# Three token tiles of the output projection moved from the token stage into the attention drain

## The reference

```python
h = s4d_kernel(x)                      # 16 sequences, 128 rows of 1024
h = concatenate([h, txt], axis=1)      # 16 x 205 rows (3280 tokens) of 1024
# attention: 32 heads of 32, one shared k and v head, alibi, causal
h = h + attn(layernorm(h)) @ Wo        # Wo 1024 x 1024
# token mixer: base layer and low rank experts with a router
x = layernorm(h)
logits = x @ router_W.T + router_b     # 15 routes
w = top 8 of softmax(logits), mapped to 8 experts
h = h + x @ base_W.T + base_b + sum_e w_e * 2 * (x @ A_e.T) @ B_e.T
```

## Time and profile before

| | before |
|---|---|
| median of 3 runs | 1673.88 us (1671.83 to 1674.54) |
| the profiled execution | 1673.85 us |
| its span, first to last instruction | 1672.1 us |
| PE busy | 1471.7 us (88%) |
| DVE busy | 1137.9 us (68%) |
| ACT busy | 735.7 us (44%) |
| POOL busy | 514.7 us (31%) |
| mean granted TensorE clock | 0.96 |
| DMA | 139.81 MB |

### The profile page before, as it was taken

One profiled execution on the slowest core, in us unless ns is written; L12 is line 12 of the kernel. 1 busy time (PEld: TensorE's weight loads), 2 busy tenths in 40 slices (PEclk: granted clock), 3 DMA queues, 4 the chain that ended last, 5 costly groups with the idle time before them and its releaser, 6 DMA issues. The chain is left out here.

```text
span 1672.1 us, 28883 instructions
## 1 busy us (share of the span) xinstructions
PE 1471.7 (88%) x9700; PEld 1315.2 (79%) x9700; DVE 1137.9 (68%) x4142; ACT 735.7 (44%) x2624; POOL 514.7 (31%) x314
## 2 busy tenths in 40 slices
PE   0264479999999999999999779999999999999999
PEld 0264478788888888887887558998999989899997
DVE  7999268989898988888879754453444435444443
ACT  3364229688787878786878631101101110111100
POOL 2687214444444444453445401010101101011010
PEclk9878789999999999999998789999999999999999
DMA  6134545546465646365555341212112121121211
GB/s 207 38 76 106 115 86 83 111 71 119 77 122 82 117 72 120 65 117 87 90 119 93 103 166 38 76 39 74 62 51 75 38 75 50 63 75 38 76 38 37
DMA packets 110522, 139.81 MB, mean 84 GB/s; under 512 B 13156, under 2 KB 96484, under 8 KB 110040
## 3 DMA queue, kind: packets, MB, share of 16 engines
q1 hardware_dynamic: 110408, 138.41, 36.8%
HBM read 62.82 MB, written 40.30 MB: 62 GB/s over the span
## 5 line engine op out<-in xcount | busy, mean ns | idle before, releaser
L735 ACT ACTIVATE P<-P,nmax 128x128 f32<-128x128 f32 (+1 forms) x1024 | 434.6, 426 | 86.3 <-DVE nmax L823 82.4
L797 POOL TENSOR_TENSOR P<-P,rden 128x512 f32<-128x512 f32 (+1 forms) x256 | 330.3, 1312 | 404.8 <-DVE rden L829 404.5
L823 DVE CUSTOM_DVE_ANT_0 P<-sc,mask 128x128 f32<-128x128 f32 (+1 forms) x1024 | 292.1, 323 | 73.1 <-PE sc L630 68.2
L1161 POOL TENSOR_TENSOR h<-h,base_b 128x1024 f32<-128x1024 f32 (+1 forms) x26 | 63.0, 2422 | 640.0 <-DVE xn L1188 640.0
L660 PE MATMUL pr<-xT_hi,wq_hi 128*128 128x410 f32 x576 | 242.8, 421 | 0.6 <-DVE xT_lo L839 0.6
L835 DVE COPY PTR<-pt 128x282 f32<-128x282 f32 x512 | 220.6, 432 | 14.2 <-PE pt L640 13.1
L1072 PE MATMUL b<-w_hi,x2T_hi 128*128 128x390 f32 (+3 forms) x624 | 214.6, 344 | 1.0 <-DVE x2T_lo L1198 1.0
L1072 PE MATMUL b<-w_lo,x2T_hi 128*128 128x390 f32 (+3 forms) x624 | 212.9, 341 | 0.0
L1072 PE MATMUL b<-w_hi,x2T_lo 128*128 128x390 f32 (+3 forms) x624 | 212.6, 341 | 0.0
L660 PE MATMUL pr<-xT_lo,wq_hi 128*128 128x410 f32 x576 | 201.4, 350 | 0.0
L660 PE MATMUL pr<-xT_hi,wq_lo 128*128 128x410 f32 x576 | 200.4, 348 | 0.0
(11 more groups left out here) (174 smaller groups left out, 3005.6 us busy)
## 6 DMA issues: line engine op xcount, KB each, us to landing
Qs<-q_hi SPq DMA_DIRECT2D x128, 205.0 KB, 4.8
Qs<-q_lo SPq DMA_DIRECT2D x64, 205.0 KB, 5.7
att_dram<-att SPq DMA_DIRECT2D x64, 205.0 KB, 2.8
at<-att_dram SPq DMA_DIRECT2D x25, 512.0 KB, 4.5
h<-h_dram SPq DMA_DIRECT2D x25, 512.0 KB, 3.4
out<-h SPq DMA_DIRECT2D x25, 512.0 KB, 2.6
h_dram<-Y SPq DMA_DIRECT2D x64, 128.0 KB, 3.0
ht<-h_dram SPq DMA_DIRECT2D x16, 512.0 KB, 6.1
```

Of the source, the lines that this page charges most:

```text
L735: last = nc.scalar.activation(P[rows, j % 2, i, cols], P[rows, j % 2, i, cols], ACT.Exp, scale=-1.0, bias=nmax[at], accum_out=den[at])
L797: lastp = nc.gpsimd.tensor_tensor(w, w, r, ALU.mult)
L823: lastv = v.tensor_tensor_reduce(P[0:n, j % 2, i, cols], sc[i % 2][0:n, cols], mask[0:n, m], 1.0, 3.0e38, ALU.add, ALU.min, nmax[0:n, j % ...
L1161: nc.gpsimd.tensor_tensor(h2[0:n, par, :], h2[0:n, par, :], base_b[0:n, :], ALU.add).then_inc(biased, 1)
```

## The change

Attention's output projection of tiles 0, 1 and 2 (384 tokens, all of them of the first two sequences) is computed in the drain of the attention block. Each of the 48 turns from turn 4 of the drain takes three matmuls of 512 columns (`out_step`); a half tile takes eight turns. For it `at` is loaded, split into `aT` (views of the buffers of xT, which are free after the last main product), the residual is loaded into `ht`, the sum is added there by DVE (`add_half`) and stored back to `h_dram`. So that Wo is there in time, it is read in column blocks, in the order of the main products, and each block is split into the place of a block of Wq that has been used: seven of the nine in the last pair, two slots behind the main product, two in the drain. The token stage goes over tiles 3 to 25 first and then over 0, 1 and 2, which skip the projection. `turn_z` stands in front of `transpose_x` in bodies without a projection, and `RESIDUAL_AFTER` is 2.

```diff
+EARLY = 3
+TILES_OUT = FULL + 1
+LATER = TILES_OUT - EARLY
...
-    WO_PIECES = KC + 1
-    SPLIT_AT = [1, 2, 3, 4] + [32, 33, 34, 35, 44]
+    WO_PIECES = len(MAIN)
+    WO_RING = 4
+    SPLIT_AT = [GH * (n + 2) + 2 for n in range(7)] + [GH * SLOTS + 2, GH * SLOTS + 5]
...
-        turn = GH * slot + i - after
-        return SPLIT_AT.index(turn) if last is None and turn in SPLIT_AT else None
+        turn = GH * slot + i - after + (GH * SLOTS if last is None else 0)
+        return SPLIT_AT.index(turn) if last in (True, None) and turn in SPLIT_AT else None
+
+    OUT_FROM, HALVES = 4, 2 * EARLY
+    A_HI_AT, A_LO_AT = [0, 12, 28], [1, 14, 30]
+    RES_SLOT = [1, 2, 3]
+    aT = [[w[:, :, r * 128:(r + 1) * 128] for w in xT] for r in range(2)]
...
+            def load_wo(n):
+                if n >= WO_RING:
+                    sp.wait_ge(wo_lo, n - WO_RING + 1)
+                if MAIN[n] == "kv":
+                    src = io["BT"].rearrange("p (k m) -> p k m", k=KC)
+                else:
+                    j = MAIN[n][1]
+                    src = io["Wo"].rearrange("(k p) m -> p k m", p=128)[:, :, 128 * j:128 * j + 128]
+                sp.dma_start(wo_stage(n), src).then_inc(wo_loaded[n], 16)
...
+            def store_res(t):
+                sp.wait_ge(half_read, 2 * t + 2)
+                sp.dma_start(io["h_dram"][t * 128:(t + 1) * 128, :], ht[:, RES_SLOT[t], :]).then_inc(res_stored, 16)
...
+                    if last is True and 3 <= slot < 3 + WO_PIECES - WO_RING:
+                        load_wo(slot + WO_RING - 3)
+                    if last is True and slot == 6:
+                        for q in att_stored:
+                            sp.wait_ge(q, 16 * 2 * UNITS // 2)
+                        for t in range(2):
+                            load_at(t, t, ta_loaded[t])
+                    if last is True and slot == 8:
+                        sp.wait_ge(wo_lo, 6)
+                        load_res(0)
                     if last is None and slot == 1:
...
+                        sp.wait_ge(ta_lo, 1)
+                        load_at(2, 0, ta_loaded[2])
+                        sp.wait_ge(wo_lo, 8)
+                        for t in (1, 2):
+                            load_res(t)
+                    if last is None and slot == 3:
+                        store_res(0)
+                        sp.wait_ge(ta_lo, 2)
+                        load_at(EARLY + 1, 1, W["a_loaded"][1])
                     if last is None and slot == 5:
...
+                        store_res(1)
+                        sp.wait_ge(ta_lo, 3)
+                        load_at(EARLY, 0, W["a_loaded"][0])
...
+            store_res(2)
+            sp.wait_ge(res_stored, 16 * EARLY)
...
+            def out_step(half, k):
+                t = half // 2
+                if k == 0:
+                    if half % 2 == 0:
+                        pe.wait_ge(ta_lo, t + 1)
+                    if half < 2:
+                        pe.wait_ge(wo_lo, (5, WO_PIECES)[half])
+                    if half < BANKS:
+                        pe.wait_ge(main_read, SLOTS * PAIRS - 2 + half)
+                    else:
+                        pe.wait_ge(half_read, half - BANKS + 1)
+                cols = slice(512 * (half % 2), 512 * (half % 2) + 512)
+                for m, (a, b) in enumerate(((0, 0), (0, 1), (1, 0))):
+                    last = nc.tensor.matmul(pr[half % BANKS][:, 0:512], aT[t % 2][a][:, k, :], wq[b][:, k, cols],
+                                            start=(k == 0 and m == 0), stop=(k == KC - 1 and m == 2))
...
+            def add_half(half):
+                t, cols = half // 2, slice(512 * (half % 2), 512 * (half % 2) + 512)
+                dve.wait_ge(half_done, half + 1)
+                dve.wait_ge(res_loaded[t], 16)
+                v.tensor_tensor(ht[:, RES_SLOT[t], cols], pr[half % BANKS][:, 0:512], ht[:, RES_SLOT[t], cols], ALU.add).then_inc(half_read, 1)
...
-    RESIDUAL_AFTER = 4
+    RESIDUAL_AFTER = 2
...
-                if n1 and not first:
+                ahead = n1 and not first and attends(t + 1)
+
+                def turns():
+                    if not ahead:
+                        turn_z(t, n)
+                    if n1:
+                        transpose_x(t + 1, n1, 0)
+                if ahead:
                     attn_out(t + 1, 1 - par, n1, between=lambda: turn_z(t, n))
                 wait_count(pe, out_ready, t)
                 three(base_ps[1], n, xT, w2, slice(*CHUNKS[1]), KC, stop=False)
-                if first or not n1:
-                    turn_z(t, n)
-                three(base_ps[2], n, xT, w2, slice(*CHUNKS[2]), KC, stop=False, between_at=TURN_AT,
-                      between=(lambda: transpose_x(t + 1, n1, 0)) if n1 else None)
+                three(base_ps[2], n, xT, w2, slice(*CHUNKS[2]), KC, stop=False, between_at=TURN_AT, between=turns)
```

More of the change, by code:

```diff
@@ L468, in attention_block @@
     rows_ready = sem("rows_ready")
+    ta_loaded, res_loaded = [sem(f"ta_loaded{i}") for i in range(EARLY)], [sem(f"res_loaded{i}") for i in range(EARLY)]
+    ta_hi, ta_lo, half_done, half_read, res_stored = sem("ta_hi"), sem("ta_lo"), sem("half_done"), sem("half_read"), sem("res_stored")
     wo_hi, wo_lo = sem("wo_hi"), sem("wo_lo")
@@ L718, in body @@
                             main_step(p, slot, main, i)
+                        if last is None and out_half(slot, i)[0] is not None:
+                            out_step(*out_half(slot, i))
                         chunk, pair = ln_chunk(slot, i, 0), ln_pair(p, slot, first, last)
@@ L737, in exp_head, with a_hi @@
                 last.then_inc(exp_done, 1)
+            def a_hi(t):
+                act.wait_ge(ta_loaded[t], 16)
+                if t >= 2:
+                    act.wait_ge(half_done, 2 * (t - 1))
+                nc.scalar.activation(aT[t % 2][0], W["at"][:, t % 2], ACT.Copy).then_inc(ta_hi, 1)
             def hi_ln(p, i):
@@ L773, in body @@
                             act.wait_ge(wo_loaded[k], 16)
-                            nc.scalar.activation(part_of(W["wq_hi"], k), ht[:, k % 4, :], ACT.Copy).then_inc(wo_hi, 1)
+                            nc.scalar.activation(part_of(W["wq_hi"], k), wo_stage(k), ACT.Copy).then_inc(wo_hi, 1)
+                        if last is None and GH * slot + i in A_HI_AT:
+                            a_hi(A_HI_AT.index(GH * slot + i))
                         if i == 6 and aj is not None:
@@ L905, in body @@
                             dve.wait_ge(wo_hi, k + 1)
-                            v.tensor_tensor(part_of(W["wq_lo"], k), ht[:, k % 4, :], part_of(W["wq_hi"], k).bitcast(F32),
+                            v.tensor_tensor(part_of(W["wq_lo"], k), wo_stage(k), part_of(W["wq_hi"], k).bitcast(F32),
                                             ALU.subtract).then_inc(wo_lo, 1)
+                        if last is None and GH * slot + i in A_LO_AT:
+                            a_lo(A_LO_AT.index(GH * slot + i))
+                        if last is None and out_half(slot, i, 1)[1] == KC - 1:
+                            add_half(out_half(slot, i, 1)[0])
                         if i == RECIP_AT[1] and tj is not None:
@@ L1014, in mlp_block @@
     out_stored = [sem("out_stored0"), sem("out_stored1")]
-    LAST = FULL
     def visit(eng, body):
-        size = lambda t: 128 if t < FULL else (REST if t == FULL else 0)
-        pairs = (FULL - 2) // 2
-        for t in range(2):
-            body(t, t % 2, t // 2, 128, 128, 128)
+        size = lambda u: 0 if u > FULL else (REST if u == LATER - 1 else 128)
+        pairs = (LATER - 3) // 2
+        for u in range(2):
+            body(u, u % 2, u // 2, 128, 128, 128)
         with eng.Fori(1, pairs) as i:
@@ L1025, in visit, with attends, row0 @@
                 body(i * 2 + par, par, i, 128, 128, 128)
-        for t in range(2 * pairs, FULL + 1):
-            body(t, t % 2, t // 2, size(t), size(t + 1), size(t + 2))
+        for u in range(2 * pairs, FULL + 1):
+            body(u, u % 2, u // 2, size(u), size(u + 1), size(u + 2))
+    def attends(u):
+        return not isinstance(u, int) or u < LATER
+    def row0(u):
+        return ((u + EARLY) if attends(u) else (u - LATER)) * 128
     with nc.Block() as block:
@@ L1224, in body @@
             def body(t, par, half_t, n, n1, n2):
-                link = Chain(dve, chain, LINKS * t + (5 + RSQRT_LINKS), setup)
+                fewer = 0 if attends(t) else t + 1 - LATER
+                link = Chain(dve, chain, LINKS * t + (5 + RSQRT_LINKS) - fewer, setup)
                 router(t, n, link)
```

55 lines of the change are left out of this document (30 added, 25 removed).

## The result

The changed kernel runs at **1686.2 us** (median of 4 runs, 1684.47 to 1689.79) against 1674.2 for the kernel before on the same chip: 1.0074 times its time, 95% interval 1.0062 to 1.0087. Forecast were 1677.8 and, as the range, 1668.5 to 1684.0. Of faster, same and slower, slower had the highest chance; the size was wrong, and the time lies outside the range.

A forecast was written before the change was run, and what follows sets the result against it. The prediction took PE's chain, mostly base product `b` and output projection `wo`, as the bound. Last pair 3.5, drain 12.1, start 1.2, projections -33.6, tail gaps 16.2 and clock 4.5 sum to +3.9: 1677.8 us, range 1668.5 to 1684.

The forecast's parts named there:

- Last pair: Slots 2 to 8 of attention's last pair: seven early Wo splits cost 0.5 us each, +3.5 us.
- 8.2 as the upper bound: Last pair: seven splits at 2.21 us, each us of DVE work lengthening the slot by 0.53, give 8.2 us.
- Rival (c): Last pair: splits stretch against POOL, each taking 2.21 us, pair grows by 8.2; 1682.5 us; chance 0.10.
- Drain: Attention's drain to the first `wo`, with 48 projection steps and turns of 1.16 us: +12.1 us.
- 0.5 for `a_lo` in DVE's order: Drain: 0.5 us added to PE's end for the place of `a_lo` in DVE's order.
- (d): Drain: the low clock stays, a turn takes about 2.0 us instead of 1.16; 1685 us; chance 0.10.
- (e): Drain: projection steps don't use idle PE, all 33.6 us come on top; 1699 us; chance 0.02.
- Start of the token stage: First `b` 3.2 us earlier, low clock +1.7, later `turn_z` of the first tile +2.7: net +1.2 us.
- Tail: Token stage's last three tiles with non-attending successors: 5.4 us PE idle each, +16.2 us, and low clock behind, +4.5.
- (a): Drain and new gaps: the clock isn't lost, taking back 8.8 us; 1669.0 us, faster; chance 0.18.
- (b): Last pair: DVE's 1.50 us idle per slot hide all splits; 1674.3 us; chance 0.15.
- the gain of 33.6 us: Token stage: three projections fewer at 11.2 us of PE each, -33.6 us.

The follow-up runs named there:

- split at turn 1: Changed kernel with DVE's low split of each Wo piece five turns later, at turn 1 of the next slot: 1687.4 us, 1.0079 of the kernel before.
- the run with `turn_z` early: Changed kernel with turn_z between the second and last third of the base product in bodies without a projection: 1673.3 us, 0.9994 of the kernel before.
- the run with the splits alone: Changed kernel without the projection in the drain, token stage as before, early Wo loads and splits kept: 1677.3 us, 1.0020 of the kernel before.
- the run with halves: Changed kernel with each low Wo split on DVE cut into two halves, the second two turns later: 1684.2 us, 1.0060 of the kernel before.
- statistics early: Changed kernel with `turn_z` early, plus layernorm statistics of a next tile without projection before DVE's wait for zT: 1664.1 us, 0.9932 of the kernel before.
- three edits: Changed kernel with low splits on GpSimd, `turn_z` early and next tile's layernorm statistics before the wait for zT: 1656.1 us, 0.9887 of the kernel before.

## Why the prediction was wrong

**Last pair, the step that failed.** "I take 0.5 us each, 3.5", with 8.2 as the upper bound; measured 9.9. Two things were wrong in it. The sum of DVE's work ("the sum of the DVE work fits": 1.50 us idle, a split of 1.47) is not the test: of DVE's 1.50 us idle in slot 2 of before, 1.36 lie ahead of the bias of turn 7, the split in the middle of a dense row of biases and copies, and what counts is whether PE's lead of two heads covers the instruction. I had named this lead and priced it at half a microsecond; a split of 1.2 us costs 0.84 (split at turn 1), and the run with the splits on GpSimd shows that nothing else costs anything by itself. And the upper bound took 0.53 us of slot per us of DVE from layernorm statistics one pair earlier, which are many short instructions; a single long one costs 1.35/1.88, 0.72 per us.

Rival (c), at 0.10, had one half of the mechanism, the stretch beside POOL: with the measured 9.9 in place of its 8.2 its 1682.5 becomes 1684.2, but no split took the 2.21 us that it gave to each (1.23 to 1.88), and it left out the cost without a stretch. DVE's timeline of before, the idle time of slot 2 and the split of 2.21 us:

```profile
850.72 0.29 DVE L823 CUSTOM_DVE_ANT_0 P<-sc,mask 128x128 f32<-128x128 f32 x1 [1.36 <-PE sc L630]
...
947.93 2.21 DVE L906 TENSOR_TENSOR wq_lo<-ht,wq_hi 128x1024 fp32r<-128x1024 f32 x1
```

I had read that split as lying in POOL's 3.54 us. It didn't: POOL ended at 949.06, the split at 950.14, 1.08 us later, so the rows of before already showed the wait that the last section works out.

Slots 6 and 7 carry 4.5 of the 9.9: in slot 6 the split waited 0.97 us for ACT, which I had put at 0.05 us free, and PE's granted clock was 0.88, and 0.95 in slot 7. That clock loss in the pair wasn't in my sum at all. The trace shows it beside the waits; no run separates it from them.

**Drain.** +12.1 forecast, +10.2 measured. A turn of 1.16 us (930.45 to 931.68 is one of 1.23; the next are 1.15 to 1.17), the first step 5.2 us after `q_hi`, 6.2 from PE's end to `wo`: each step within 0.3 us of the forecast. The low clock held for two turns of 1.78 and 2.10 us (922.98 to 924.76 to 926.86), 1.6 us over 1.16 each, not 2.6; of the 0.5 for `a_lo` in DVE's order nothing shows. Rivals (d) and (e) have fallen.

**Start of the token stage.** +1.2 forecast, +3.4 measured. The first `b` came 2.6 us earlier (forecast 3.2), `turn_z` cost 2.7 (the gap is 6.69 instead of 4.02) as forecast; the clock behind the gap of 5.07 us cost 2.5 in place of 1.7 (by the run with RESIDUAL_AFTER 4), and 0.8 lie behind the longer second gap. (My own times gave 996.4 - 990.5 = 5.9 us idle ahead of `b`, not the 5.5 written; measured 5.07.)

**Tail.** The three gaps: 15.6 us, forecast 16.2 (0.82 + 4.70 less the transpose's 0.27 is 5.25 each, not 5.4). What is left, -10.8 + 33.6 - 15.6 = 7.2, forecast 4.5, is the clock behind them but for some 0.6: from the transposes to the next `zp` it took 17.53, 18.01 and 16.54 us, against 12.52 and 15 more matmuls (2.7), 15.2, behind the gap in the run with `turn_z` early that kept its clock; that is 2.4, 2.8 and 1.4. I had priced the nine matmuls alone (2.91 instead of 1.6, right for two of the three); the eight transposes around them take 1.11 and 0.85 instead of 0.44 each, 1.1 us more behind each of those two.

**The sum.** 9.9 + 10.2 + 3.4 - 10.8 = 12.7 against 3.9: 6.4 of the error is the last pair, 2.2 the start, 2.1 the tail, less 1.9 in the drain. All clock terms but the drain's were too small: a gap slows everything behind it, not the rows that one happened to read. Rivals (a) and (b) have fallen.

Where did the gain of 33.6 us go? 19.6 us went into the drain, which takes 50.74 once the splits have left it; 22.8 into the tail's gaps and their clock; 3.9 into the start, against the run with the splits alone (63.5 from the first `wo` to the one behind `b`, 59.7 there). Together 46.3 for 33.6: as written the projection loses, and the early splits give the +9.9 for the 9.4 that the drain gets back. These are stretches of profiled executions; by the medians the splits alone cost 3.3 us and the projection 8.9 more.

## What to carry to other kernels

Before work is put into the idle time of an engine, look where in the slot that time lies and which copy or mask will stand behind the new instruction; if the critical engine needs something from that queue before the new instruction has ended, the sum of busy time does not tell whether it fits. A matmul that is taken away also takes the cover of what ran beside it: here the layernorm of the next tile, which could be moved ahead of the wait by cutting it in two. Side work can go to an engine that nobody waits for even at half the speed (2.38 us instead of 1.2): here that took the pair from 71.89 to 62.09 us.

## What the runs showed of the hardware

In these traces a subtraction with both inputs in SBUF does not run slower beside GpSimd's multiplication, it stands still until one of GpSimd's instructions ends. In the changed kernel POOL's pair of instructions ends at 848.60 + 2.56 = 851.16; the split of 850.37 ended at 852.25, 1.09 us later, and one alone takes 1.23. The split of 870.92 began only 0.27 us ahead of POOL's end (868.63 + 2.56 = 871.19) and ended at 872.28, again 1.09 us behind it: the rest is the same however much of POOL's instruction was left. In the run with halves POOL ended at 845.36 + 2.56 = 847.92, and the half ended at 848.47, 0.55 later, where one alone takes 0.68. The second half made POOL's pair take 3.01 instead of 2.56. DVE's copies from PSUM (0.44) and its bias (0.28 and 0.36) took the same beside POOL as without it. The Trainium skill, SBUF — State Buffer, SBUF: two separate sides, says that the port pair shared by VectorE and GpSimd is an exclusive lock, held for the whole instruction, and that the other one waits; these rows agree with it. An estimate taken from it, that a split meeting one GpSimd instruction lasts at most that instruction longer (1.55 us for the longer of POOL's pair), would have held: 0.66 us more were seen.

Of TensorE's clock: after gaps of 5.1 to 6.7 us the transposes took 1.11 or 1.12 us each time, the lower level. After gaps of 2.5 to 2.6 us, in the run with `turn_z` early, they took 1.11 once and 0.66 twice, but behind one of the latter the clock fell 0.9 us later (0.50 from 1629 to 1631): two of the three gaps lost it. Behind a gap of 4.02 us the same transposes took 0.82 (before), 1.12 (statistics early) and 0.66 (three edits), and in the last of these too the clock was at 0.50 from 1030 us on, 1.4 us behind the gap's end: the first matmuls do not tell whether a gap cost the clock. Behind one gap of 2.37 and all gaps of 0.95 us or less in the tail the clock stayed at 1.00. So shortening the gaps made the loss smaller and rarer, and at 2.5 us not impossible.
